# Three cross-attention stages: 18 of 24 probability blocks turned by VectorE and DMA instead of TensorE

## The reference

```python
q_hk  = (x @ Wq.T).reshape(8, 56, 16, 128)
q_big = einsum('bshk,hkq->bshq', q_hk, w_kc_q)        # layers 0 and 2: then a rotary embedding
q_r   = einsum('bshq,hqr->bhsr', q_big, W_qr)
k_r   = einsum('bld,hdr->bhlr', rope(ctx), W_kr)
scores = einsum('bhsr,bhlr->bhsl', q_r, k_r)
attn  = softmax(scores, axis=-1)                      # over 1500 context rows
ctx_c = einsum('bhsl,bld->bhsd', attn, rope(ctx))     # 64 features
out   = (einsum('bhsd,hkd->bhsk', ctx_c, w_kc_kv)) @ Wo.T
x     = layernorm(x + out)
```

## Time and profile before

| | |
|---|---|
| median of 3 runs | 1666.74 us (1664.62 to 1668.67) |
| profiled execution, its own time as the profile gives it: the span from the first to the last instruction | 1666.3 us |
| PE busy in the span | 1627.4 us (98%) |
| DVE busy | 1113.9 us (67%) |
| ACT busy | 749.9 us (45%) |
| POOL busy | 239.1 us (14%) |
| granted TensorE clock, mean | 0.992 of full speed |

### The profile page before, as it was taken

One profiled execution on the slowest core, in us unless ns is written; L12 is line 12 of the kernel. 1 busy time (PEld: TensorE's weight loads), 2 busy tenths in 40 slices (PEclk: granted clock), 3 DMA queues, 4 the chain that ended last, 5 costly groups with the idle time before them and its releaser, 6 DMA issues.

```text
span 1666.3 us, 35653 instructions
## 1 busy us (share of the span) xinstructions
PE 1627.4 (98%) x15234; PEld 1104.8 (66%) x15234; DVE 1113.9 (67%) x1974; ACT 749.9 (45%) x1297; POOL 239.1 (14%) x428
## 2 busy tenths in 40 slices
PE   9999999999999899999999999999999999999998
PEld 5575367777755666655377777764566767777765
DVE  3735899999566763266899999435445289999623
ACT  2223366666413641144366666312444366666411
POOL 0011300000010313011200000010455000000030
PEclk9999999999999999999999999999999999999999
DMA  8302020000040011051020000050300220000010
GB/s 280 86 13 83 1 78 2 2 2 2 2 187 1 2 59 40 1 133 48 1 97 2 2 2 2 4 240 0 64 1 1 114 89 2 2 2 2 2 44 11
DMA packets 35522, 71.10 MB, mean 43 GB/s; under 512 B 25359, under 2 KB 29775, under 8 KB 31433
## 3 DMA queue, kind: packets, MB, share of 16 engines
q1 hardware_dynamic: 35240, 68.71, 12.6%
q10 hardware_dynamic: 126, 0.11, 0.0%
HBM read 68.36 MB, written 0.46 MB: 41 GB/s over the span
## 4 chain that ended last, share of the span: by engine, by line
PE 89%; DVE 6%; ACT 2%; POOL 1%; issue 1%; DMA 1%; SPq 0%; DVEq 0%; POOLq 0%; ACTq 0%
PE ps L1122 14%; PE ps L1135 14%; PE ps L1035 13%; PE ps L1501 9%; PE ps L361 9%; PE ps L946 3%; PE ps L2599 3%; PE ps L1150 3%; PE ps L528 2%; PE ps L1961 2%; PE ps L956 1%; POOL arena L1795 1%; PE ps L2626 1%; PE ps L982 1%; PE ps L967 1%
## 5 line engine op out<-in xcount | busy, mean ns | idle before, releaser
L1236 ACT ACTIVATE arena<-ps,softmax_stats 128x1500 f32<-128x1500 f32 x168 | 253.8, 1511 | 193.0 <-DVE softmax_stats L1317 190.8
L1135 PEld LDWEIGHTS ps<-arena,ctx_pos 125*64 125x64 f32 x4608 | 222.3, 137 | 58.4 <-issue 55.4
L1122 PE MATMUL ps<-ident,arena 64*125 64x64 f32 x4032 | 239.1, 271 | 1.9 <-ACT arena L1236 1.6
L1135 PE MATMUL ps<-arena,ctx_pos 125*64 125x128 f32 (+1 forms) x4608 | 240.5, 262 | 0.0
L1122 PEld LDWEIGHTS ps<-ident,arena 64*125 64x125 f32 x4032 | 226.8, 185 | 17.0 <-issue 13.5
L1035 PE MATMUL ps<-ctx_feat,arena 64*128 64x500 f32 x1008 | 230.5, 590 | 0.0
L1243 ACT COPY arena<-ps 125x512 f32<-125x512 f32 x336 | 172.5, 600 | 77.9 <-PE ps L1122 77.9
L1315 DVE TENSOR_REDUCE softmax_stats<-ps 128x1 f32<-128x500 f32 x252 | 170.6, 678 | 49.0 <-PE ps L1035 48.6
L361 PE MATMUL ps<-arena 128*128 128x256 f32 x736 | 174.7, 383 | 3.5 <-DVE arena L1630 1.2
L1328 DVE TENSOR_SCALAR arena<-arena,softmax_stats 128x1500 f32<-128x1500 f32 x168 | 168.3, 1002 | 5.9
L1501 PE MATMUL ps<-x_feat,arena 128*128 128x448 f32 (+1 forms) x416 | 167.9, 549 | 1.2 <-DVE arena L1613 1.2
(11 more groups left out here) (324 smaller groups left out, 1931.7 us busy)
## 6 DMA issues: line engine op xcount, KB each, us to landing
ctx_pos<-in_ctx SPq DMA_DIRECT2D x1, 2688.0 KB
arena<-in_L1f_gate SPq DMA_DIRECT2D x1, 2304.0 KB, 12.1
arena<-in_L1f_up SPq DMA_DIRECT2D x1, 2304.0 KB, 17.0
arena<-in_L1f_down SPq DMA_DIRECT2D x1, 2304.0 KB, 7.8
arena<-in_L0a_Wq SPq DMA_DIRECT2D x1, 2048.0 KB, 10.9
arena<-in_L0a_Wc SPq DMA_DIRECT2D x1, 2048.0 KB, 18.8
arena<-in_L0x_Wq SPq DMA_DIRECT2D x1, 2048.0 KB, 9.9
arena<-in_L0x_Wo SPq DMA_DIRECT2D x1, 2048.0 KB, 8.3
```

The lines of the kernel that those rows point to most:

```text
L1122: m = nc.tensor.transpose(c.ps[0:LP, turn_bank(i, k, r), n * 64:(n + 1) * 64], probs[i % 2][e][rows, l * LP:(l + 1) * LP], c.ident[rows, r ...
L1135: m = nc.tensor.matmul(y[r * 64:(r + 1) * 64, lo:hi], c.ctx_pos[:, j, l, e, :], pT[i % 2][:, lo // 64:hi // 64, LT * e + l, :], start=(l = ...
L1236: nc.scalar.activation(probs[i % 2][e].rearrange("p (k l) -> p k l", k=3), sc[e], ACT.Exp, bias=low[:, i % 4, e:e + 1], accum_out=total[:, ...
```

## The change

The normalisation of the probabilities goes. The exponentials write their blocks 128 apart (`LQ`; 125 are used), and 18 of the 24 blocks (all 12 of e = 0, the last 6 of e = 1) no longer go through PE:

- `turn_blocks(i, e)` on DVE transposes 32 x 32 blocks inside each group of 32 partitions, 1536 columns for e = 0 and 768 for e = 1, into `blocks[i % 2]`.
- SP then moves each of the 4 x 4 partition groups to where it belongs, 16 SBUF to SBUF transfers of 32 partitions x 576 columns (2304 bytes a row) for each unit, into `moved_to[i % 2]`.
- `turn(i)` on PE transposes the 6 blocks that are left (12 transposes), into half of the columns used before; ACT copies them out in two operations of 384 columns.
- `weigh(i)` takes 18 of its moving operands from `moved_to` as four runs of 32 columns.

The division by the row sum moves behind `weigh`: DVE takes one reciprocal for both batches, POOL makes two 128 x 128 diagonal tiles of it (`spread_out`), PE spreads them over 64 partitions with two matmuls (`spread`), ACT copies the product out (`keep_spread`), and POOL multiplies where it copied (`place_context`, up to three units later). `keep` moves from DVE to ACT.

The exponential of e = 1 becomes two operations, banks 0 and 1 (1000 columns), then bank 2 (500), each with its own row sum; DVE adds the sums. `score(i, 0)` now waits for the first of the two and `score(i, 2)` for the second. The loads of the next stage move from SP to ACT, behind unit 0's exponentials.

The diff, cut to its core:

```diff
-    pT = [c.at(o["PT"] + i * LT * 256, LT * 256, LP)...  for i in range(2)]
-    probs = [[c.at(o["P"] + (2 * i + e) * L, L) for e in range(2)] for i in range(2)]
+LQ, BY_PE = 32 * 4, 6
+RUN = 32 * (2 * LT - BY_PE)
+    blocks = [c.at(o["TT"][i], 4 * RUN).rearrange("p (g n) -> p g n", g=4) for i in range(2)]
+    moved_to = [c.at(o["PT"] + i * 4 * RUN, 4 * RUN).rearrange("p (g n) -> p g n", g=4) for i in range(2)]
+    probs = [[c.at(o["P"] + (2 * i + e) * LT * LQ, LT * LQ) for e in range(2)] for i in range(2)]
...
     def _(sp):
-        sp.wait_ge(lat_in.handle, lat_in.at(4 * NH // 2))
-        prefetch(sp)
+        for i in range(NU):
+            sp.wait_ge(blocked[1].handle, blocked[1].at(i + 1))
+            if i >= 2:
+                sp.wait_ge(pv_mm.handle, pv_mm.at(i - 1))
+            for frm in range(4):
+                for to in range(4):
+                    sp.dma_start(moved_to[i % 2][32 * to:32 * to + 32, frm, :],
+                                 blocks[i % 2][32 * frm:32 * frm + 32, to, :]).then_inc(moved[i % 2].handle, 16)
...
+        def spread_out(i):
+            pool.wait_ge(recip.handle, recip.at(i + 1))
+            for e in range(2):
+                nc.gpsimd.tensor_scalar(diag[i % 2][:, e, :], c.ident[:], inv[:, i % 4, e:e + 1], 1.0, ALU.mult, ALU.mult)
+        def place_context(i):
+            for r, e, lo, hi in parts(u):
+                nc.gpsimd.tensor_tensor(ctxT[rows, 2 * j + e, at + lo:at + hi], held[i % 2][rows, lo:hi],
+                                        rinv[i % 2][rows, lo:hi], ALU.mult).then_inc(*ct_in.next())
...
             if i > 0 and k == 0:
-                for e in range(2):
-                    pe.wait_ge(exped[e].handle, exped[e].at(i))
+                pe.wait_ge(exped[0].handle, exped[0].at(i))
+                pe.wait_ge(exped[1].handle, exped[1].at(2 * i - 1))
+            if i > 0 and k == 2:
+                pe.wait_ge(exped[1].handle, exped[1].at(2 * i))
...
         def weigh(i):
+            pe.wait_ge(moved[i % 2].handle, moved[i % 2].at(256 * (i // 2 + 1)))
+            if i > 0:
+                pe.wait_ge(kept.handle, kept.at(i))
...
-            for k in turn_order(i - 1):
-                turn(i - 1, k)
+            turn(i - 1)
+            spread(i - 1)
...
+            nc.scalar.activation(to[:, 0:2], frm[:, 0:2], ACT.Exp, bias=low[:, i % 4, 1:2],
+                                 accum_out=total[:, i % 4, 1:2]).then_inc(*exped[1].next())
+            nc.scalar.activation(to[:, 2], frm[:, 2], ACT.Exp, bias=low[:, i % 4, 1:2],
+                                 accum_out=rest[:, i % 4:i % 4 + 1]).then_inc(*exped[1].next())
...
+        for i in range(NU + 2):
+            if i >= 3:
+                keep(i - 3)
+            if i >= 2:
+                copy_turned(i - 2, 0)
+                copy_turned(i - 2, 1)
+                keep_spread(i - 2)
             if i < NU:
                 exp(i, 0)
                 exp(i, 1)
             if i == 0:
...
+                prefetch(act)
...
-            nc.vector.tensor_scalar(probs[i % 2][e], probs[i % 2][e], inv[:, i % 4, e:e + 1], None,
-                                    ALU.mult).then_inc(*normed[e].next())
+        def turn_blocks(i, e):
+            dve.wait_ge(exped[e].handle, exped[e].at((1 + e) * (i + 1)))
+            if i >= 2 and e == 0:
+                dve.wait_ge(moved[i % 2].handle, moved[i % 2].at(256 * (i // 2)))
+            n = BY_PE * e
+            nc.vector.transpose(blocks[i % 2]...,
+                                probs[i % 2][e]...).then_inc(*blocked[e].next())
...
+        for i in range(NU):
+            rowmax(i)
+            turn_blocks(i, 0)
+            turn_blocks(i, 1)
+            invert(i)
```

More of the change, by code:

```diff
@@ L848, in score_order @@
         return (2, 1, 0) if i == 0 else (0, 1, 2)
-    def turn_order(i):
-        return (2, 0, 1) if i == 0 else (0, 1, 2)
     def big3_bank(p):
@@ L1102, in _, with turn @@
         out_of_context(3)
[L1104 to L1113, removed]
+        def turn(i):
+            pe.wait_ge(exped[1].handle, exped[1].at(2 * i + 1))
+            if i == 0:
@@ L1114, in turn @@
                 pe.wait_ge(lat_in.handle, lat_in.at(4 * NH // 2))
                 pe.wait_ge(cm_act.handle, cm_act.at(3))
-            if k == (1 if i == 0 else 2) and i < NU - 1:
-                pe.wait_ge(exped[1].handle, exped[1].at(i + 2))
-            for n in range(8):
-                e, l = divmod(8 * k + n, LT)
+            else:
+                pe.wait_ge(b_in.handle, b_in.at(2 * i))
+                pe.wait_ge(rinv_in.handle, rinv_in.at(i))
+            for l in range(BY_PE):
                 for r in range(2):
@@ L1125, in turn, with spread @@
                         m.then_inc(*(turned_hi if r else turned_lo).next())
+        def spread(i):
+            pe.wait_ge(diag_in.handle, diag_in.at(2 * i + 2))
+            for r, e, lo, hi in parts(i % UNITS):
+                m = nc.tensor.matmul(spread_ps[r * 64:(r + 1) * 64, lo:hi], ones, diag[i % 2][:, e, lo:hi], start=True, stop=True,
+                                     skip_group_check=True)
+            m.then_inc(*spread_mm.next())
         def weigh(i):
             j, u = i // UNITS, i % UNITS
-            pe.wait_ge(a_in.handle, a_in.at(4 * (i + 1)))
@@ L1134, in weigh @@
                 for r, e, lo, hi in parts(u):
-                    m = nc.tensor.matmul(y[r * 64:(r + 1) * 64, lo:hi], c.ctx_pos[:, j, l, e, :],
-                                         pT[i % 2][:, lo // 64:hi // 64, LT * e + l, :], start=(l == 0 and lo == 0),
+                    if e == 1 and l < BY_PE:
+                        p = pT[i % 2][:, lo // 64:hi // 64, l, :]
+                    else:
+                        at = 32 * (LT * e + l - BY_PE * e)
+                        p = moved_to[i % 2][0:LP, lo // 32:hi // 32, at:at + 32]
+                    m = nc.tensor.matmul(y[r * 64:(r + 1) * 64, lo:hi], c.ctx_pos[:, j, l, e, :], p, start=(l == 0 and lo == 0),
                                          stop=(l == LT - 1), skip_group_check=True)
@@ L1170, in _ @@
         project(1)
-        for k in range(3):
-            turn(NU - 1, k)
+        turn(NU - 1)
+        spread(NU - 1)
         project(2)
@@ L1235, in exp @@
                 act.wait_ge(wide_in.handle, wide_in.at(4))
-            nc.scalar.activation(probs[i % 2][e].rearrange("p (k l) -> p k l", k=3), sc[e],
-                                 ACT.Exp, bias=low[:, i % 4, e:e + 1],
-                                 accum_out=total[:, i % 4, e:e + 1]).then_inc(*exped[e].next())
-        def copy_turned(i, k, r):
-            done = turned_hi if r else turned_lo
-            act.wait_ge(done.handle, done.at(3 * i + turn_order(i).index(k) + 1))
-            nc.scalar.copy(pT[i % 2][:, r, 8 * k:8 * k + 8, :],
-                           c.ps[0:LP, turn_bank(i, k, r), :].rearrange("p (s q) -> p s q", s=8)).then_inc(*a_in.next())
@@ L1246, in _ @@
-        for i in range(NU + 1):
+            to = probs[i % 2][e].rearrange("p (k l q) -> p k l q", k=3, l=4)[:, :, :, 0:LP]
+            frm = sc[e].rearrange("p k (l q) -> p k l q", l=4)
+            if e == 0:
+                nc.scalar.activation(to, frm, ACT.Exp, bias=low[:, i % 4, 0:1],
+                                     accum_out=total[:, i % 4, 0:1]).then_inc(*exped[0].next())
+                return
+            nc.scalar.activation(to[:, 0:2], frm[:, 0:2], ACT.Exp, bias=low[:, i % 4, 1:2],
+                                 accum_out=total[:, i % 4, 1:2]).then_inc(*exped[1].next())
```

133 lines of the change are left out of this document (69 added, 64 removed).

## The result

The changed kernel takes 1882.32 us (median of 4 runs, 1876.74 to 1886.89), the kernel before beside it 1667.70 (4 runs): a ratio of 1.1274, 95% interval 1.1233 to 1.1315. The forecast was 1620 us; the kernel became 214.6 us slower.

A forecast was written before the change was run, and what follows sets the result against it. PE bound the kernel before, at 8.13 us a unit; SP's issuing would bind at 7.5. 24 x (8.13 - 7.5) = 15.1, -1 + 1.5: 15.6 us a stage, 47 for three, giving 1620 us, range 1585 to 1715.

The forecast's parts named there:

- 16 x 0.47 = 7.5 us a unit: SP's queue in the loop: 16 transfer issues a unit, one after another, 0.47 us each; longer than DVE/ACT and PE work.
- Rival C: SP's 32-row issues alternate between 0.42 and 0.58 us, 8.8 us a unit, 48 us more, 1715 us; chance 0.21.
- The start: Start of each stage's loop: weigh(0) waits for transfers sharing DMA engines with the next weights, +1 us (0 to 5).
- The ends of the loop: End of each stage's loop: two turns save 2.00 us each on PE, unit 26's transfers are awaited; -1.5 us (-4 to +3).
- rival D: PE idles 1.1 us a unit and its clock falls; one fall a unit gives 8.04 us, 1660 us total; chance 0.12.
- The chain: DVE and ACT per unit: reductions, exponentials, transposes, addition and reciprocal in sequence, a period of 6.85 us.
- The 6.2 that the forecast gives for fast transposes: Period of the DVE and ACT sequence, in us, if its two transposes cost 1.02 + 0.51 us.
- PE's 6.34 us: PE's work in a steady unit: scores 2.66, weigh 2.77, remaining transposes 0.67, spreading matmuls 0.24 us.
- two signs that the forecast had named for a wrong working: PE busy over 95% of the loop, or ACT's exponentials waiting for POOL, would make the working wrong whatever the time.
- The rule that spoke against the forecast: DMA initiation is usually small against transfer: 2.7 us a unit at 435 GB/s, SP hidden, the 6.85 us DVE/ACT period decides.

## Why the prediction was wrong, point by point

The spans differ by 213.9 us. The three long windows hold 757.6 - 585.6 = 172.0 of it, the three starts 29.8 (100.4 less 3 x 23.53), and all the rest 12.1.

- **The step that failed**: "I take 0.47 us, 16 x 0.47 = 7.5 us a unit; the range is 0.42 to 0.63 us, 6.7 to 10 us a unit". Measured: 0.669 from issue to issue, 10.7 us of issuing a unit. That SP would be the bound was right; the term was 3.2 us a unit too small. The value came from loads out of HBM; a transfer inside SBUF is 0.17 us longer to issue (0.59 against 0.42, by itself and in the loop), and the single long issues, which the forecast had no term for, add most of another 0.6 us a unit (16 x 0.036). The text said that no row shows such a transfer, and still took a value near the lower end of its range. Even the upper end was passed. The trace of before held a warning: 32 loads out of HBM that follow one another on SP's queue, two of them long, take 0.576 us each, and by that row sixteen issues need 9.2 us, more than the 8.13 of the kernel before.

```profile
727.75 18.44 SPq L125 DMA_DIRECT2D arena<-in_L2x_kcq  x32
```

- **Rival C** had the right side and the right place, and a wrong mechanism: the issues don't change between 0.42 and 0.58 by turns, nearly all take the longer time.
- **The start**, "+1 us a stage (0 to 5)", cost 9.2 to 10.6. Weigh(0) waits for transfers that share the DMA engines with the weights. In the timeline of the start, ACT issues these from 211.59 on, SP its first transfers at 212.39:

```profile
211.59 0.38 ACTq L125 DMA_DIRECT2D arena<-in_L0f_gate  x1
...
212.39 24.18 SPq L896 DMA_DIRECT2D arena<-arena  x36
...
228.18 5.39 PE L1175 MATMUL ps<-arena,ctx_pos 125*64 125x128 f32 x48 [6.41 <-DMA arena<-arena]
```

  With the weights moved to unit 8 the start was 5.3 us shorter. With the weights behind the loop and fewer issues nothing of the loss was left in the first stage. In the changed kernel most of this loss is made up later, though: SP issued through the first start without a wait, the scores gained 5.7 us on SP over the 24 units behind it, and the whole was no shorter with the weights at unit 8.
- **The ends of the loop**, -1.5 us a stage: the rest is 12.1 us to the slow side for three stages. Most of it, 9.7 us, lies between the second and the third loop (299.6 us from unit 27 to unit 0, before 289.9). There the granted clock is 0.68 in one stretch, at the same distance behind the second loop at which it was 1.00 before. The changed kernel with one exponential, whose edit doesn't touch that stretch, kept 1.00 as well. The rows are of the changed kernel, the kernel before and the one with one exponential:

```profile
1438.90:1458.90 20.00, 19.15 (x109) 16.96 (x106) 3.35 (x6) 1.12 (x3) 0.00 (x0) 0.68 0.53 222
1305.80:1325.80 20.00, 19.15 (x128) 15.72 (x128) 2.45 (x4) 4.25 (x13) 0.00 (x0) 1.00 0.45 190
1440.40:1460.40 20.00, 19.06 (x176) 16.31 (x172) 3.93 (x6) 4.80 (x13) 0.00 (x0) 1.00 0.60 238
```

  With one exponential the way from loop to loop took 293.6 us, so some 6 of the 9.7 us go with this fall (half the bytes, where the clock fell too: 300.4 us; late weights, where it didn't: 291.9). Why it fell in one kernel and not in the other stayed open. Without it some 6 us are left for three stages: the gain that the forecast saw at the ends of the loop did not show.
- **The clock, rival D**, came true as a companion: 0.89 in the loops, where weigh waits for transfers, and 1.00 in the loop with eight issues, where it doesn't. PE's busy time in the loop is 185.8 us against 161.7 there, so the lower clock stretches its work by 24 us a stage. SP has no wait in the first loop, so there this lies in PE's waits and lengthens nothing; in the other stages it was not separated. The Trainium skill, TensorE: Matmul & The Clock Gate, the section on HAM oscillation, describes this pattern, bursts of matmuls with waits for a DMA between them, and the trace agrees.
- **The chain**, "a period of 6.85 us": that 6.81 was measured with eight issues is luck, because PE set that time, and not the chain. A steady unit took 6.74 there, so the chain needs no more than that; its own period was not measured. The 6.2 that the forecast gives for fast transposes doesn't follow from its terms: the second exponential ends at 5.57, and 0.51 and 0.3 behind it make 6.4. The chain's terms, by shape in the changed kernel (count, busy us, mean ns):

```profile
L1392 DVE STREAM_TRANSPOSE arena<-arena 128x1536 f32<-128x1536 f32 x84 | 149.4, 1778 | 73.6 <-DMA arena<-arena 67.1 <-PE ps L970 4.1 <-ACT arena L1277 0.4
...
L1280 ACT ACTIVATE arena<-ps,softmax_stats 128x1000 f32<-128x1000 f32 x84 | 92.6, 1103 | 1.7
L1392 DVE STREAM_TRANSPOSE arena<-arena 128x768 f32<-128x768 f32 x84 | 80.4, 957 | 3.1
...
L1282 ACT ACTIVATE arena<-ps,softmax_stats 128x500 f32<-128x500 f32 x84 | 56.6, 673 | 0.0
```

  The transposes were taken as 1.76 and 0.95 us and took 1.78 and 0.96; the exponentials as 1.05 and 0.59, and took 1.10 and 0.67. The row nearest in size had nearly the right price for the transposes; as it is of another operation, that is luck too.
- **PE's 6.34 us** was 0.40 too low, and PE is the next bound behind SP. With eight issues its unit is 2.72 (scores), 2.77 (weigh), 0.80 (the 12 transposes, forecast 0.67) and 0.45 (the spreading, forecast 0.24), 6.74 us from start to start. So two signs that the forecast had named for a wrong working came out once SP was out of the way: PE is busy for 99% of that window, and ACT's last copy ahead of its exponentials waits for POOL in almost every unit, 54.6 us in all:

```profile
ACT arena L1304 <- POOL arena L933: 54.6, 23, 2.8
```

  In the changed kernel SP's issuing hides both.
- **The rule that spoke against the forecast.** The Trainium skill, DMA: Bandwidth & Descriptors, the section on issuing engines that are not separate DMA queues, has the time to initiate a DMA usually small against the transfer. Here the measurement decides otherwise: half the bytes changed nothing, half the issues took the wait away.

The forecast had the bound by name and priced it with rows of another kind. As the sign turned inside the stated range (from 0.51 us an issue on), the price of that one operation deserved the greater part of the doubt.

## What to carry to other kernels

When work is handed to DMA, count the issues before the bytes: between SBUF and SBUF each takes its queue 0.6 to 0.7 us here, whatever it moves. A term that stands 16 times in the sum has to be priced with a row of the same kind, source and destination included, and over a run of them, so that the long ones are in it, or forecast at the slow end of its bounds. And before issues are shared out to a second queue, look for the wait that already fills that engine's gap: the same idea gave 1796 us behind the wait and 1580 ahead of it, with two issues in place of four and four transfers replaced by copies (how much of this the place alone gives was not tried).

## What the runs showed of the hardware that was not expected

- Into SBUF, an issue took 0.42 to 0.43 us with the source in HBM (32 and 128 rows of 448 bytes) and 0.59 to 0.60 with the source in SBUF (16 to 128 rows, 448 to 1792 bytes a row), by the medians. ACT's queue took 2.46 us for four inside SBUF. Neither is a rule for all shapes: three stores from SBUF to HBM took 0.32 to 0.39, and a load of 32 rows from HBM 0.58.
- Some issues take 1.0 to 1.9 us: 15 of 375 in the first loop of the changed kernel, 14 of 190 in that with eight issues a unit, 9 of the 128 that were measured by themselves; why was not tried.
- A 32 x 32 transpose of 1536 float32 columns on DVE takes 1.78 us, one of 768 columns 0.96.
- POOL copied 32 partitions x 576 columns in 0.66 us, about what passed from issue to issue on SP (0.67), and DVE's transposes of 1536 columns stayed at 1.78 us beside it.
